# Experts' second weights: a load from HBM by SP in place of a copy on chip by GpSimd

## The chip, the cores and the metric

One core of one Trainium2 chip. The metric is the device time of one launch in microseconds (us), median of several runs. Engines are named as in the profile: PE (TensorE, matmuls), PEld (its weight loads), DVE (VectorE), ACT (ScalarE), POOL (GpSimd) and SP (SyncE, which here only issues DMAs).

## The reference

One layer in float32 over x (2, 1024, 256). A convolution and delta-rule attention with a gate over five paths comes first, then a gated recurrence over the 1024 steps gives h for 2048 tokens. The change lies in the last part, a feed-forward layer of eight experts, of which each token takes one:

```python
logits = xf @ gate_w.T + gate_b
top1 = jnp.argmax(logits, axis=-1)
for e in range(n_experts):                # 8
    h = jax.nn.relu(xf @ w1[e].T + b1[e])  # w1[e]: 1024 x 256
    y = h @ w2[e].T + b2[e]                # w2[e]: 256 x 1024
    out = out + jnp.where((top1 == e)[:, None], y, 0)
x = x + out
```

## The kernel before

The parts run one after the other, each a block of programs, one per engine, tied by semaphores written out by hand. `recur` (from about 599 us) computes h, and SP loads during it the experts' first weights `m.w1` (eight DMAs of 1 MB, line 1593) and two of the second ones `m.w2` (line 1595), and near its end four more of w2 (line 1603). All weights of all eight experts lie in SBUF when the blocks of tokens run.

`experts` (from 760.6 us) sorts the tokens by expert. DVE works out each token's place, PE turns h into rows, ACT copies them to `row` (line 2031), and SP writes the 16 tiles of rows to HBM as `h_rows` (line 1879), each when ACT has it. The sorted tokens are cut in 20 blocks (`BLOCKS`) of 128. A block has two halves of 64 tokens, and each half has one expert, whose number stands in `eid_i[0, 2g]` and `eid_i[0, 2g+1]` (cast at line 2117). The token list, `slot_token`, is cast at line 2124.

For block g:

- POOL gathers 128 rows of h (`fetch_x`, line 1908) and of the residual (`fetch_z`, line 1916) by indirect DMAs, and scatters the result (line 1929).
- PE turns the gathered rows (`turn_in`, line 1971), DVE copies them to `xt` (line 2139).
- PE computes the hidden layer (`hidden`, lines 1982 and 1985): per 512 columns and 128 inputs two matmuls that run side by side, tokens of the first half against `m.w1` at a register's expert, tokens of the second half against `w1_copy[g % 2]`, a room of one expert's weights in the tile h, which is no longer needed when h has been turned.
- DVE copies the hidden layer (line 2146), PE turns it (`turn_hidden`, line 2008), ACT applies bias and relu (line 2041), PE computes the output (`output`, lines 1996 and 1999), whose second half reads `w2_copy[g % 2]`, copied by DVE (line 2133). DVE adds residual and bias (lines 2154 and 2157).

`w1_copy` has two buffers. POOL fills them by `copy_w1(g)` (line 1893): wait until hidden(g-2) is done, load the expert's number into a register, copy 128 x 2048 floats from `m.w1`. PE's `hidden(g)` waits for `w1_copied` to reach g+1. The order on PE is hidden(g), turn_in(g+1), output(g-1), turn_hidden(g). The order on POOL is, once per g: fetch_x(g+3), copy_w1(g+2), wait for y of block g, scatter(g), fetch_z(g+2). Ahead of the loop stand copy_w1(0), the waits for the token list and for all rows of h in HBM, fetch_x(0), fetch_x(1), fetch_z(0), fetch_z(1), fetch_x(2), copy_w1(1). SP has nothing to do after the last row of h. DVE's first copy_w2 also waits for the rows in HBM. `keep_clock` is a helper (line 50) that gives PE matmuls of no use while it would wait.

Of the kernel before, what the change touches and what calls it, by code (L numbers as in the profile page):

```python
# [19 lines left out]
P = 128  # L20
# [15 lines left out]
E, EH = 8, 1024  # L36
# [3 lines left out]
BLOCKS = (B * T // HALF + E) // 2  # L40
# [1764 lines left out]
def experts(nc, d, m, out):  # L1805
# [9 lines left out]
    TILES = TOK // P  # L1815
    K2 = EH // P
    with ExitStack() as own:  # L1817
        sb = lambda n, s: own.enter_context(nc.sbuf_tensor("moe_" + n, s, F32))
        sem = lambda n: m.whole.enter_context(nc.semaphore("moe_" + n))
# [25 lines left out]
        eid_i = own.enter_context(nc.sbuf_tensor("eid_i", [1, 2 * BLOCKS], I32))  # L1845
        row = free_zw.rearrange("p (a n) -> p a n", n=D)
        w2_copy = free_zw[:, 0:2 * K2 * D].rearrange("p (i k n) -> p i k n", i=2, k=K2)
        w1_copy = m.h[:].rearrange("p j t -> p (j t)")[:, 0:2 * C * EH].rearrange("p (i c n) -> p i c n", i=2, c=C)
# [11 lines left out]
        names = ("zeros", "rows_out", "cleared", "r", "count_psum", "slots_ready", "slot_psum",  # L1860
                 "tokens_ready", "eid_ready", "turned", "row_ready", "picked", "x_psum", "xt_ready", "hid_psum", "hid_ready",
                 "ht_psum", "ht_ready", "y_psum", "y_half", "y_ready",
                 "w1_copied", "w2_copied")
        s = namedtuple("ExpertSemaphores", names)(*(sem(n) for n in names))
        x_in = [sem(f"x_in{i}") for i in range(2)]
        z_in = [sem(f"z_in{i}") for i in range(2)]
        y_done = [sem(f"y_done{i}") for i in range(2)]
        TURNED, TURNED_LAST = 2, 2
        out_rows = out.rearrange("b t d -> (b t) d")
# [3 lines left out]
        @block.sync  # L1873
        def _(sp):
            for e in (W2_AHEAD + 2, W2_AHEAD + 3):
                sp.dma_start(w2[:, e], d.w2T[e].rearrange("(k p) n -> p k n", p=P)).then_inc(m.w2_in, 16)
            for a in range(TILES):
                sp.wait_ge(s.row_ready, a + 1)
                sp.dma_start(m.h_rows[a * P:(a + 1) * P, :], row[:, a, :]).then_inc(s.rows_out, 16)

        @block.gpsimd
        def _(pool):
            for x in (*xin, *zin):
                nc.gpsimd.memset(x[:], 0.0).then_inc(s.cleared, 1)
            pool.wait_ge(s.cleared, 4)

            def copy_w1(g):
                if g >= BLOCKS:
                    return
                if g >= 2:  # L1890
                    pool.wait_ge(s.hid_psum, 2 * (g - 1))
                e = pool.value_load(eid_i[0:1, 2 * g + 1:2 * g + 2], min_val=0, max_val=E - 1)
                nc.gpsimd.tensor_copy(w1_copy[:, g % 2], m.w1[:, bass.ds(e, 1)].rearrange("p o c n -> p (o c) n")).then_inc(s.w1_copied, 1)

            pool.wait_ge(s.turned, TILES)
            pool.wait_ge(s.eid_ready, 1)
            copy_w1(0)
            pool.wait_ge(s.tokens_ready, 1)
            pool.wait_ge(s.rows_out, 16 * TILES)

            slots = lambda g: bass.IndirectOffsetOnAxis(ap=slot_token[:, g:g + 1], axis=0)

            def fetch_x(g):
                if g >= BLOCKS:
                    return
                if g >= 2:
                    pool.wait_ge(s.x_psum, g - 1)
                nc.gpsimd.indirect_dma_start(out=xin[g % 2][:], out_offset=None, in_=m.h_rows, in_offset=slots(g),
                                             bounds_check=TOK - 1, oob_is_err=False).then_inc(x_in[g % 2], 16)

            def fetch_z(g):
                if g >= BLOCKS:
                    return
                if g >= 2:
                    pool.wait_ge(s.y_half, g - 1)
                nc.gpsimd.indirect_dma_start(out=zin[g % 2][:], out_offset=None, in_=m.z_rows, in_offset=slots(g),
                                             bounds_check=TOK - 1, oob_is_err=False).then_inc(z_in[g % 2], 16)

            fetch_x(0)
            fetch_x(1)  # L1920
            fetch_z(0)
            fetch_z(1)
            fetch_x(2)
            copy_w1(1)
            for g in range(BLOCKS):
                fetch_x(g + 3)
                copy_w1(g + 2)
                pool.wait_ge(s.y_ready, 2 * (g + 1))
                nc.gpsimd.indirect_dma_start(out=out_rows, out_offset=slots(g), in_=y[g % 2][:], in_offset=None,  # L1929
                                             bounds_check=TOK - 1, oob_is_err=False).then_inc(y_done[g % 2], 16)  # L1930
                fetch_z(g + 2)
            for i in range(2):
                pool.wait_ge(y_done[i], 16 * ((BLOCKS + 1 - i) // 2))

        @block.tensor
        def _(pe):
# [36 lines left out]

            def hidden(g, e):
                pe.wait_ge(s.xt_ready, g + 1)
                pe.wait_ge(s.w1_copied, g + 1)
                for n in range(EH // N):
                    cols = slice(n * N, (n + 1) * N)
                    if g:
                        pe.wait_ge(s.hid_ready, 2 * (g - 1) + n + 1)  # L1980
                    for c in range(C):
                        nc.tensor.matmul(hid_bank[n][side(0), :], xt[:, c, side(0)],  # L1982
                                         m.w1[:, bass.ds(e, 1), c, cols].rearrange("p o n -> p (o n)"),
                                         start=(c == 0), stop=(c == C - 1), skip_group_check=True)
                        last = nc.tensor.matmul(hid_bank[n][side(1), :], xt[:, c, side(1)], w1_copy[:, g % 2, c, cols],  # L1985
                                                start=(c == 0), stop=(c == C - 1), skip_group_check=True)
                    last.then_inc(s.hid_psum, 1)
# [25 lines left out]

            turn_in(0)
            hidden(0, expert(0))
            turn_in(1)
            turn_hidden(0)
            pe.wait_ge(m.w2_in, 16 * (E - W2_AHEAD))
            for g in range(1, BLOCKS):
                hidden(g, expert(g))  # L2020
                if g + 1 < BLOCKS:
                    turn_in(g + 1)
                output(g - 1, expert(g - 1))
                turn_hidden(g)
# [186 lines left out]
def layer_kernel(nc, ins, out):  # L2211
    d = namedtuple("Inputs", ins)(**ins)
    with ExitStack() as ctx:
# [64 lines left out]
        m.h_rows = nc.dram_tensor("h_rows", (B * T, D), F32).ap()  # L2278
        recur(nc, d, m)
        experts(nc, d, m, out)  # L2280

# [35 lines left out]
```

## Time and profile before

| | us |
|---|---|
| median of 3 runs | 965.83 |
| lowest and highest | 963.97, 968.57 |
| the profiled execution | 969.41 |
| its span, first to last instruction | 967.6 |
| mean granted clock of PE, share of full | 0.873 |
| PE busy | 719.3 (74%) |
| DVE busy | 681.5 (70%) |
| ACT busy | 531.1 (55%) |
| POOL busy | 284.4 (29%) |
| DMA, mean over the span | 63 GB/s |

The profile is of one execution. Busy shares are means over the span, and here the parts of the kernel have different limits. So it is read by stretch: a table of stretches tells which engine is full, the chain that ended last tells what that stretch waits for, and the instructions in order of time tell how early each thing is ready. Times below are us from the start of the span.

### The profile page before, as it was taken

The page shows a single profiled execution, that of the slowest core. Times are in us where ns is not written, and L with a number is a line of the kernel's source. Part 1 is how long each engine was busy: PE and PEld are TensorE (multiplying, and loading weights), DVE is VectorE, ACT ScalarE, POOL GpSimd, SP SyncE. Part 2 cuts the span into 40 slices and gives each one's busy share as a digit, 9 for nine tenths or more (in the row PEclk, how much of TensorE's full clock was granted, in tenths as well). Part 3 has the DMA queues.
Part 4 walks back from the last instruction along what each step waited for, and adds up shares of the span by engine and source line. Part 5 has one row for each costly group of instructions (what it writes and reads, how often), then busy time and mean ns, then how long its engine had stood idle before and what let it go on. Part 6 is the DMA issues. An engine that isn't in the chain of part 4 may idle for free. (4 is left out here: it accounts for less than half of the span.)

```text
span 967.6 us, 16500 instructions
## 1 busy us (share of the span) xinstructions
PE 719.3 (74%) x6146; PEld 419.8 (43%) x6146; DVE 681.5 (70%) x958; ACT 531.1 (55%) x978; POOL 284.4 (29%) x238
## 2 busy tenths in 40 slices
PE   3850008886766547786598697999998989999995
PEld 1320004432545547775354254444444844445542
DVE  4999985967844798446679782799999734545442
ACT  5888854653423433555445345999999214443332
POOL 0000000000201000000033400699999156566661
PEclk9985557988899758899788899999999699999998
DMA  5640000000894000100300002920000911111100
GB/s 203 217 143 0 0 0 23 1 0 0 223 245 97 4 2 3 25 3 3 111 1 1 11 22 78 393 83 0 1 0 1 337 42 46 39 43 36 45 26 6
DMA packets 35473, 60.78 MB, mean 63 GB/s; under 512 B 7771, under 2 KB 22107, under 8 KB 35010
## 3 DMA queue, kind: packets, MB, share of 16 engines
q1 hardware_dynamic: 32514, 53.42, 17.6%
q0 software_dynamic: 2880, 6.30, 2.2%
q8 instruction: 50, 0.82, 0.4%
q14 instruction: 29, 0.24, 0.1%
HBM read 54.46 MB, written 6.82 MB: 63 GB/s over the span
## 5 line engine op out<-in xcount | busy, mean ns | idle before, releaser
L2041 ACT ACTIVATE xT<-x_tr,moe_b 128x64 f32<-128x64 f32 x320 | 67.6, 360 | 115.5 <-PE x_tr L2008 115.5
L1982 PE MATMUL x_hid<-w,moe_xt 128*64 x160 | 74.6, 610 | 0.8 <-DVE moe_xt L2139 0.6
L1985 PE MATMUL x_hid<-h,moe_xt 128*64 128x512 f32 x160 | 74.6, 610 | 0.0
L1996 PE MATMUL x_y<-w,xT 128*64 x320 | 73.3, 382 | 1.8 <-ACT xT L2041 1.8
L1999 PE MATMUL x_y<-hs,xT 128*64 128x256 f32 x320 | 73.3, 382 | 0.0
L1756 DVE TENSOR_TENSOR_SCAN w<-r_bank,w 128x512 f32<-128x512 f32 x56 | 69.6, 1246 | 3.2 <-POOL w L1716 3.2
L1170 POOL TENSOR_TENSOR path<-path,mix_pr 128x1280 f32<-128x1280 f32 x12 | 28.7, 2421 | 132.9 <-DVE mix_pr L1405 132.9
L224 PE MATMUL bad_sum<-spike_bad,ones 128*128 128x16 f32 x2 | 0.6, 384 | 83.9 <-ACT spike_outside L190 83.9
L1624 PE MATMUL r_bank<-recur_h_other,w1h 128*128 128x512 f32 x128 | 60.2, 592 | 0.2 <-ACT recur_h_other L1665 0.2
L1618 PE MATMUL r_bank<-hs,eye 128*128 128x512 f32 x112 | 57.2, 592 | 1.2 <-PEq L1099 1.2
L1716 POOL TENSOR_TENSOR w<-w,recur_h_other 128x512 f32<-128x512 f32 x32 | 37.7, 1180 | 65.6 <-ACT recur_h_other L1665 59.6
L220 PE MATMUL w_bank<-spike_wbuf,spike_pick 128*128 128x512 f32 x80 | 39.5, 654 | 23.4 <-DMA spike_wbuf<-in_gW 23.4
L482 DVE SCALAR_TENSOR_TENSOR proj_y<-proj_pre,mix_st,proj_y 128x1024 f32<-128x1024 f32 x36 | 46.2, 1285 | 11.0 <-ACT proj_y L445 9.8
L1996 PEld LDWEIGHTS x_y<-w,xT 128*64 128x64 f32 x320 | 42.3, 137 | 25.7 <-issue 5.6
L2154 DVE TENSOR_TENSOR moe_y<-x_y,moe_zin 128x256 f32<-128x256 f32 x20 | 8.5, 425 | 60.9 <-PE x_y L1999 60.9
L397 PE MATMUL pj<-hs,mix_st 128*128 128x512 f32 x96 | 46.3, 629 | 2.3 <-PEq L72 2.3
L2146 DVE COPY xT<-x_hid 128x512 f32<-128x512 f32 x40 | 27.7, 691 | 28.1 <-PE x_hid L1985 28.1
L1929 POOL DMA_INDIRECT out<-moe_y,slot_token x20 | 26.6, 1328 | 65.0 <-DVE moe_y L2157 65.0
L1624 PE MATMUL r_bank<-h,w1h 128*128 128x512 f32 x96 | 45.1, 592 | 0.0
L656 DVE COPY path<-fir_z_bank 64x256 f32<-64x256 f32 x64 | 27.0, 422 | 25.0 <-PE fir_z_bank L591 23.4
L419 POOL MEMSET proj_pre<- 128x6 f32 x1 | 0.1, 104 | 146.1 <-POOLq L72 146.1
L1688 ACT ACTIVATE r_bank<-r_bank,recur_leak,recur_leak_neg 128x512 f32<-128x512 f32 x56 | 42.0, 751 | 1.9
(297 smaller groups left out, 2006.4 us busy)
## 6 DMA issues: line engine op xcount, KB each, us to landing
spike_wbuf<-in_gW SPq DMA_DIRECT2D x8, 1280.0 KB, 6.4
w<-in_w1T SPq DMA_DIRECT2D x8, 1024.0 KB, 12.1
w<-in_w2T SPq DMA_DIRECT2D x8, 1024.0 KB, 9.0
fir_band<-in_band_l SPq DMA_DIRECT2D x11, 512.0 KB
fir_band<-in_band_m SPq DMA_DIRECT2D x11, 312.0 KB
mix_st<-in_band_l SPq DMA_DIRECT2D x5, 512.0 KB
xT<-in_xT SPq DMA_DIRECT2D x4, 512.0 KB, 6.4
xT<-in_xT SPq DMA_DIRECT2D x2, 1024.0 KB, 6.2
```

Source lines behind the costliest of these rows:

```text
L220: last = nc.tensor.matmul(w_bank[:], pick[:, at:at + P], wbuf[:, ch % 2, i, :], start=(ch == 0 and i == 0), stop=(ch == CHUNKS - 1 and i = ...
L397: last = nc.tensor.matmul(pj[u % 2][:, n * N:(n + 1) * N], w[:, i, k, c * P:(c + 1) * P], m.hs[:, k * B + b, n * N:(n + 1) * N], start=(k ...
L482: nc.vector.scalar_tensor_tensor(out, pre[:, u % 2, k:k + T], wc[:, i, c, k:k + 1], out, ALU.mult, ALU.add).then_inc(conv_step if k < KQ - ...
L1618: nc.tensor.matmul(out, m.eye[:], zw[:, c * B + b, t0:t0 + N], start=True, stop=False)
L1624: last = nc.tensor.matmul(out, wg[:, k, c * P:(c + 1) * P], state[u // UNITS % 2][:, k * B + b, t0:t0 + N], start=False, stop=(k == C - 1))
L1688: nc.scalar.activation(out, out, ACT.Identity, bias=leak[:, c:c + 1], scale=leak_neg[:, c:c + 1]).then_inc(s.j_ready, 1)
L1756: nc.vector.tensor_tensor_scan(change[:, r, :], j_bank[u % RING][:], rest[:, r, :], first, ALU.mult, ALU.add).then_inc(s.change_ready, 1)
L1982: nc.tensor.matmul(hid_bank[n][side(0), :], xt[:, c, side(0)], m.w1[:, bass.ds(e, 1), c, cols].rearrange("p o n -> p (o n)"), start=(c == ...
L1985: last = nc.tensor.matmul(hid_bank[n][side(1), :], xt[:, c, side(1)], w1_copy[:, g % 2, c, cols], start=(c == 0), stop=(c == C - 1), skip_ ...
L1996: nc.tensor.matmul(y_bank[side(0), :], ht[:, k, side(0)], w2[:, bass.ds(e, 1), k, :].rearrange("p o n -> p (o n)"), start=(k == 0), stop=( ...
L1999: last = nc.tensor.matmul(y_bank[side(1), :], ht[:, k, side(1)], w2_copy[:, g % 2, k, :], start=(k == 0), stop=(k == K2 - 1), skip_group_c ...
L2041: nc.scalar.activation(ht[:, k, side(x)], turned[:, side(x)], ACT.Relu, bias=b1[:, bass.ds(e[x], 1), k]).then_inc(s.ht_ready, 1)
```

## The change

POOL's `copy_w1` is taken out. SP, after its last row of h, waits until h has been turned and the experts' numbers are there, and then for each of the 20 blocks waits until hidden(g-2) is done, loads the number of the second half's expert into a register, and issues a DMA of that expert's whole w1 (256 x 1024 floats, 1 MB) from HBM to `w1_copy[g % 2]`. `w1_copied` becomes two semaphores, one per buffer, each raised by 16 per DMA, and PE waits on the one of its buffer. `m.w1`, read by the first half, is still loaded as before.

```diff
+        w1_copied = [sem(f"w1_copied{i}") for i in range(2)]
...
         @block.sync
...
+            sp.wait_ge(s.turned, TILES)
+            sp.wait_ge(s.eid_ready, 1)
+            for g in range(BLOCKS):
+                if g >= 2:
+                    sp.wait_ge(s.hid_psum, 2 * (g - 1))
+                e = sp.value_load(eid_i[0:1, 2 * g + 1:2 * g + 2], min_val=0, max_val=E - 1)
+                sp.dma_start(w1_copy[:, g % 2], d.w1T[bass.ds(e, 1)].rearrange("o (c p) n -> p (o c) n", p=P)).then_inc(w1_copied[g % 2], 16)
 
         @block.gpsimd
...
-            def copy_w1(g):
-                if g >= BLOCKS:
-                    return
-                if g >= 2:
-                    pool.wait_ge(s.hid_psum, 2 * (g - 1))
-                e = pool.value_load(eid_i[0:1, 2 * g + 1:2 * g + 2], min_val=0, max_val=E - 1)
-                nc.gpsimd.tensor_copy(w1_copy[:, g % 2], m.w1[:, bass.ds(e, 1)].rearrange("p o c n -> p (o c) n")).then_inc(s.w1_copied, 1)
-
-            pool.wait_ge(s.turned, TILES)
-            pool.wait_ge(s.eid_ready, 1)
-            copy_w1(0)
             pool.wait_ge(s.tokens_ready, 1)
             pool.wait_ge(s.rows_out, 16 * TILES)
...
             fetch_x(2)
-            copy_w1(1)
             for g in range(BLOCKS):
                 fetch_x(g + 3)
-                copy_w1(g + 2)
                 pool.wait_ge(s.y_ready, 2 * (g + 1))
...
             def hidden(g, e):
                 pe.wait_ge(s.xt_ready, g + 1)
-                pe.wait_ge(s.w1_copied, g + 1)
+                pe.wait_ge(w1_copied[g % 2], 16 * (g // 2 + 1))
```

## Rows read from the trace of the kernel before

**Rows 1.** The page, part 1: busy time, share of the span, instructions.

```profile
PE 719.3 (74%) x6146; PEld 419.8 (43%) x6146; DVE 681.5 (70%) x958; ACT 531.1 (55%) x978; POOL 284.4 (29%) x238
```

**Rows 2.** A stretch of four blocks: its length, engines' busy us, PEclk, DMA share, GB/s.

```profile
834.00:868.00 34.00, 34.00 (x234) 17.26 (x232) 16.51 (x29) 13.20 (x65) 21.11 (x16) 1.00 0.15 44
```

**Rows 3.** Chain that ended last: start us, us, what; hidden(2), (8), (9).

```profile
798.39 0.57 PE x_hid L1982
...
849.87 0.57 PE x_hid L1982
...
858.45 0.57 PE x_hid L1982
```

**Rows 4.** Waits from 800 us on: engine, line, releaser; us, times, longest.

```profile
POOL out L1929 <- DVE moe_y L2157: 65.0, 20, 7.6
...
PE x_y L1996 <- ACT xT L2041: 1.8, 1, 1.8
```

**Rows 5.** Chain that ended last, from the last row of h to hidden(0).

```profile
772.46 4.06 DMA h_rows<-hs
...
777.48 4.10 DMA moe_xin<-h_rows,slot_token
...
782.73 0.82 PE x_hid L1982
```

**Rows 6.** Start of the experts, in order of time: start, us, instruction [idle before].

```profile
761.76 11.15 SPq L1879 DMA_DIRECT2D h_rows<-hs  x16
...
772.66 0.17 DVE L2117 CAST eid_i<-moe_eid 1x40 int32<-1x40 f32 x1
774.20 1.89 POOL L1893 COPY h<-w 128x2048 f32 x1 [12.52 <-issue]
...
774.97 1.16 DVE L2124 CAST slot_token<-moe_empty 128x20 int32<-128x20 f32 x1
...
777.48 2.24 POOL L1908 DMA_INDIRECT moe_xin<-h_rows,slot_token  x1 [1.39 <-DMA h_rows<-hs]
...
781.71 0.41 PE L1971 MATMUL x_x<-eye,moe_xin 128*128 128x128 f32 x2 [2.67 <-DMA moe_xin<-h_rows,slot_token]
```

**Rows 7.** Stretch of hidden(0), columns as in rows 2.

```profile
783.00:786.00 3.00, 3.00 (x10) 0.85 (x8) 1.12 (x1) 0.00 (x0) 2.69 (x3) 0.51 0.25 74
```

**Rows 8.** One block, in order of time: DVE's y(5) to copy(8).

```profile
840.31 0.42 DVE L2154 TENSOR_TENSOR moe_y<-x_y,moe_zin 128x256 f32<-128x256 f32 x1 [2.95 <-PE x_y L1999]
...
844.80 0.44 PE L1971 MATMUL x_x<-eye,moe_xin 128*128 128x128 f32 x2
845.59 1.01 POOL L1908 DMA_INDIRECT moe_xin<-h_rows,slot_token  x1 [0.31 <-issue]
846.60 1.90 POOL L1893 COPY h<-w 128x2048 f32 x1
```

**Rows 9.** Loads of 1 MB: issue ns and landing, of w1, then landing of w2.

```profile
L1593 SPq DMA_DIRECT2D w<-in_w1T x8: 434/484/2298, 603.5 to 608.2; - x8
...
DMA to landing us min/median/max: 5.1/12.1/18.2
...
DMA to landing us min/median/max: 5.4/8.0/10.7
```

**Rows 10.** Stretches with those loads, columns as in rows 2.

```profile
610.00:615.00 5.00, 5.00 (x13) 2.25 (x12) 2.11 (x3) 3.91 (x7) 3.34 (x4) 1.00 1.03 419
625.00:630.00 5.00, 5.00 (x13) 2.27 (x12) 4.93 (x7) 4.75 (x9) 4.63 (x5) 1.00 1.08 357
```

**Rows 11.** PE's matmuls of 512 columns, 605 to 634, then 800 to 950.

```profile
L1624 PE MATMUL r_bank<-h,w1h x21: 590/592/593, 620.7 to 633.6; 128*128 128x512 f32 x21
...
L1985 PE MATMUL x_hid<-h,moe_xt x141: 592/592/643, 799.7 to 947.2; 128*64 128x512 f32 x141
```

**Rows 12.** Stretches around the first gather, columns as in rows 2.

```profile
774.00:775.00 1.00, 1.00 (x11) 1.00 (x11) 0.39 (x3) 0.00 (x0) 0.80 (x1) 1.00 0.86 283
...
780.00:781.00 1.00, 0.00 (x0) 0.00 (x0) 0.00 (x0) 0.00 (x0) 0.98 (x1) 1.00 0.48 127
```

More of the change, by code:

```diff
@@ L1862, in experts @@
                  "ht_psum", "ht_ready", "y_psum", "y_half", "y_ready",
-                 "w1_copied", "w2_copied")
+                 "w2_copied")
         s = namedtuple("ExpertSemaphores", names)(*(sem(n) for n in names))
```

## The prediction

> **What bounds the kernel now.** The page comes first: TensorE (PE) is busy 74% of the span, GpSimd (POOL) 29% [rows 1]. An average over stages decides nothing, so I read the stage that the diff touches, the experts, which run from 760.6 us to the end. The table by stretch shows PE busy for all of a stretch of four blocks at full clock, with DMA at 15% [rows 2]. The chain of waits says the same: from one hidden product to the next it is PE work end to end, and hidden(g) starts every 8.58 us: hidden(8) at 849.87, hidden(9) at 858.45; from hidden(2) at 798.39 to hidden(9) there are 7 periods, 60.06 / 7 = 8.58 [rows 3]. In the waits from 800 us on, POOL waits for DVE's y (65.0 us in 20 waits), which itself follows PE, and PE's own longest wait is one of 1.8 us, near the end [rows 4]. So the 18 blocks from hidden(2) to the last cost 8.58 us each, and POOL's copies can only matter by making hidden wait, which they don't.
>
> Ahead of that lies a stretch that no engine fills, from the routing to hidden(0). There the chain goes: the last row of h to HBM, landed at 772.46 + 4.06 = 776.5; POOL's first gather at 777.48, landed 4.10 us later; transposes at 781.71; hidden(0) at 782.73 [rows 5, 6]. PE idles 2.67 us before 781.71 [rows 6], and after that its granted clock is 0.51, the lower level (1.2 of 2.4 GHz), from 783 to 786 us [rows 7].
>
> **The change part by part.**
>
> Removed from POOL: 20 copies of 128x2048, 1.9 us each [rows 6, 8], 38 us in all, with 20 waits and 20 register loads. What it frees on the path: nothing in the steady blocks. Copy(8) runs 846.60 to 848.49, hidden(8) starts at 849.87, 1.38 us later, and after each copy POOL waits for DVE's y before the scatter, 3.3 us on average [rows 3, 4, 8]. The gather x(9), the only POOL step on which PE soon waits, stands ahead of the copy in program order, at 845.59, so it doesn't move up. In the start, copy(0) runs 774.20 to 776.09, and DVE's cast of the token list takes 1.16 us beside it, where the cast of the expert numbers took 0.17 [rows 6]; without the copy the list is ready 0.99 us sooner, about 775.14. But POOL must also wait for the last row of h, landed 776.5, so this is hidden too: copy(0) ends 0.4 us before that landing. Had the rows come earlier, up to 0.99 us would be won. Sum of the removal: 0.
>
> Added to SP: 20 times a wait, a register load, and one DMA of 1 MB (1.05 million bytes). SP has nothing else after its last row of h, issued by 772.91 [rows 6], so what it waits for holds nobody up. The register load on SP isn't in the trace; POOL's, with its wait and dispatch, takes at most 774.20 - 772.83 = 1.37 us from the expert numbers to the copy [rows 6], and below nothing it can't go, being new work. Issuing takes 0.48 us at the median and 2.30 at most [rows 9].
>
> The transfer: 1.05 MB at the 357 to 419 GB/s of the stretch in which eight such loads ran [rows 10] is 2.5 to 2.9 us of data. From issue to landing those eight took 5.1 us (nothing ahead of it) to 18.2, median 12.1 (several ahead) [rows 9]. Here one is in flight at a time, or two at the start, so I take 5.1 to 8.0, the latter the median of four w2 loads [rows 9].
>
> Steady blocks: the weights of block 9 may be fetched once hidden(7) has ended. Hidden(7) is over when the transposes for block 8 start at 844.80, and hidden(9) starts at 858.45, so 13.6 us are there [rows 3, 8]. Needed: 1.37 + 0.48 + 8.0 = 9.9 us by the dear ends, 6.9 by the cheap landing. Hidden with 3.7 us to spare. Cost 0.
>
> Beside other transfers: 20.97 MB more over the stage. In a block, 1.05 MB in 8.58 us is 122 GB/s on top of 44 [rows 2], under half of the 357 to 419 seen. The gather x(9) is issued 845.59 to 846.60 [rows 8]; the first gather landed 4.10 - 2.24 = 1.86 us after the end of its issue [rows 5, 6], so x(9) lands near 848.5 and is wanted one period after 844.80, at 853.38. Should a whole weight transfer go ahead of it, 2.9 us, it lands at 851.4, still 2 us early. Cost 0. The z gather of block 7 and the scatter of block 5 stand ahead of x(9) in POOL's order and must be done when DVE adds y(7), two periods after it added y(5) at 840.31, so at 857.5 [rows 8]: some 12 us.
>
> PE reading SBUF while DMA writes it: matmuls of 128x512 took 590 to 593 ns, median 592, in the stretch with DMA full [rows 10, 11], and the same 592 in the steady blocks [rows 11]. Cost 0, bound 0.
>
> The start is where the new transfers meet the path. SP gets past the expert numbers at 772.83, so weights(0) go out between 773.0 and 774.7 and weights(1) half a microsecond behind. The queue is still draining: 283 GB/s in 774 to 775 [rows 12]. Behind that come 2.1 MB, 5.0 to 5.9 us of data; begun between 775 and 776, they last to 780 to 781.9. Weights(0) land between 779.6 (774.5 + 5.1) and 782.5 (+ 8.0), and hidden(0) wants them at 782.73: just in time; by the 12.1 us it would be 786.6, 3.9 late. The gather x(0) moves its data from about 780.4, after its issue began to yield at 780 [rows 12], so it meets the tail of weights(1). It may lose nothing, or up to the 2.9 us of one whole transfer; I take 0.8 us, nearly the time for which the two overlap (780.4 to about 781.2, near the middle of the range just given), on the assumption that two queues share the engines evenly. Weights(1) are wanted at 789.74 and land by 785.
>
> PE's clock: the half-clock stretch made four pairs of matmuls take 0.82 us each, twice what they take at full clock [rows 5, 7]: 4 x 0.82 / 2 = 1.6 us. A later x(0) lengthens the idle ahead of it. The stretch may stay (0), last as long again (+1.6) or fall elsewhere and vanish (-1.6). The nearest row, an idle of 2.67 us followed by it, says it stays: 0.
>
> Sum: 0 (steady) + 0 (copies) + 0.8 (x(0) behind weights(1)) = +0.8 us. The profiled execution took 969.41 us (span 967.6, 1.8 around it), so it would be 970.2; that execution was 3.6 above the median of the runs, 965.83, to which I add the same 0.8: **966.6 us**.
>
> On turns between queues the Trainium skill has a rule that speaks against this change (DMA: Bandwidth & Descriptors, "Queues, rings and completion order"): a DMA engine changes queues only after a whole packet, and a completion mark lands only after all earlier writes of its engine, whatever their queue. No row of before has a gather beside a load; by that rule x(0) would lose more than my 0.8 us, up to the whole remaining transfer, the second rival below.
>
> **The rivals.**
>
> 1. Weights late in every block (slower). With two buffers hidden(g) can't start before hidden(g-2) has ended plus L, the time from there to landing. While L is under 13.6 us it costs nothing; above, (L - 13.6) / 2 per block over 18 blocks. For it: the median landing of eight in a row, 12.1, with the dearest issue and load gives 12.1 + 2.30 + 1.37 = 15.8, so 1.1 x 18 = 19.6 us, 985.4 us. Against: that median had others ahead of it, the free one took 5.1. It passes 0.5% (4.8 us) from L = 14.1 on.
>
> 2. A gather waits out a whole transfer. At the start 2.9 in place of 0.8: 968.7 us. In steady blocks it stays hidden, as above. This is the mechanism by which the rule just named would act.
>
> 3. Start dearer still: weights(0) 3.9 us late, with 1.6 us of clock: 971.3 us. For it: the queue is full until 775.
>
> 4. Faster: copies were in the way after all, by the port that POOL and DVE seem to share (the cast of 1.16 us). At most 0.99 us at the start, plus 1.6 if the slow clock goes: 963.2. In the steady blocks PE waits for no one [rows 2, 4]. This can't pass 0.5%.
>
> 5. The change doesn't do what it says: the weights of expert e come to the same place in the same order, only the source differs; if a load by a register took SP's queue longer than a fixed one, it would be seen as rival 1.
>
> **How the numbers follow.** Forecast (within about 1.5 us of 966.6): 0.58. Rival 2: 0.16. Rival 3: 0.08. Rival 4: 0.08. Rival 1: 0.10. About 0.5%, 4.8 us, is what a measurement of this kernel can tell from no change. Forecast, rival 2 and rival 4 lie within it (0.82); rival 3 at +5.5 lies just outside, and its costs may come smaller, so half of it is slower (0.04); of rival 1, 0.08 is slower and 0.02 too small to tell. The three runs of before spread from 963.97 to 968.57, so a median can stray by 2 us: 0.04 of rival 4 goes to faster. Slower 0.08 + 0.04 = 0.12, faster 0.04, same 0.84. The range reaches from rival 4, 963.2 rounded down to 963.0, to rival 3, 971.3, and leaves out rival 1 and the tails.
>
> **What would show it.** Period: hidden(g) every 8.58 us in the chain; if it is longer, and PE's waits name the weights' DMA, rival 1; if they name the gather, the 2 us of slack was wrong. Landing: 5.1 to 8.0 us in the DMA view. Start: x(0) should land near 782.4 in place of 781.6, hidden(0) start 0.8 later, with no PE wait on weights(0). POOL's busy time should be 38 us less and its wait for y longer by as much. Matmuls should stay at 592 ns. The prediction is wrong if the start moves by over 5 us, or if a longer idle of PE brings a slow clock into further blocks.

## The result, and the profile after

| | before | after |
|---|---|---|
| median of 20 runs, us | 965.47 | 969.95 |
| lowest and highest | 963.79, 970.15 | 964.99, 974.14 |
| the profiled execution | 969.41 | 970.06 |
| its span | 967.6 | 967.7 |

The changed kernel takes 1.0044 times as long, 95% interval 1.0031 to 1.0058: 3.0 to 5.6 us more. Two further sets of 12 runs gave 1.0019 (0.9996 to 1.0043) and 1.0032 (1.0012 to 1.0052). Weighted by their runs the three give 1.0034, some 3.3 us. So the changed kernel is slower, by about a third of a percent; the upper end of the first interval is 0.58%.

The weights that the change moves are w1 of the expert of a block's second half; the "second weights" of the title are these, not w2.

The two profiled executions differ by far less than the medians, because the one of before was a late one of its kind (969.41 against a median of 965.47) and because parts that the change doesn't touch differ by PE's clock (from 300 to 400 us PE was granted 0.74 in the one and 0.80 in the other). So single executions are poor witnesses of the whole. What can be compared is a stretch with fixed ends: from the first count matmul of the experts (line 1948 before, 1943 after) to hidden(2), where the steady blocks begin. I call it **the start**. In the kernel before it takes 798.39 - 762.31 = 36.1 us, in the changed one 798.52 - 761.58 = 36.9.

One part of the cost lies outside every profile. The device time of a run is longer than its span: by 1.8 us on average in the kernel before, and by 2.3 us in the changed one. The profile, from first to last instruction, doesn't see these 0.5 us. They are there in all nine kernels of this document in which POOL copies no weights (2.2 to 2.3 us), and in none of the five, the kernel before among them, in which it copies some (1.8 us). What they are isn't known.

In what follows, hidden(0) is a row of eight **pairs** of matmuls, one for each half of the block's tokens, side by side. A pair takes 0.42 us at full clock and 0.84 at the lower level; the first of a block takes longer (0.64 and 1.11).

The chain that ended last, of the changed kernel, start us, us, what (beside rows 5):

```profile
771.92 4.22 DMA h_rows<-hs
...
777.13 4.90 DMA moe_xin<-h_rows,slot_token
...
798.52 0.57 PE x_hid L1977
807.10 0.57 PE x_hid L1977
```

The last row of h lands in 4.22 us, against 4.06. The first gather, x(0), takes 4.90 us, against 4.10. The period, from one hidden product to the next, is 807.10 - 798.52 = 8.58, unchanged. Instructions in order of time, of the changed kernel (beside rows 6):

```profile
761.58 0.80 PE L1943 MATMUL x_hid<-moe_hot,moe_before 128*128 128x128 f32 x2 [0.56 <-DVE moe_hot L2052]
...
774.23 0.18 DVE L2119 CAST slot_token<-moe_empty 128x20 int32<-128x20 f32 x1
777.02 1.23 DVE L2128 COPY hs<-w 128x2048 f32 x1 [2.61 <-DMA h_rows<-hs]
777.13 2.21 POOL L1905 DMA_INDIRECT moe_xin<-h_rows,slot_token  x1 [16.17 <-DMA h_rows<-hs]
...
782.17 0.41 PE L1966 MATMUL x_x<-eye,moe_xin 128*128 128x128 f32 x2 [3.85 <-DMA moe_xin<-h_rows,slot_token]
```

The cast of the token list takes 0.18 us where it took 1.16, and POOL waits 16.17 us, until the rows have landed, all the same: this saving is hidden. PE idles 3.85 us ahead of x(0), against 2.67. DVE's copy of 1.23 us, right beside the gather's issue of 2.21 us, becomes a lead below.

The steady blocks, in three views of the changed kernel: four blocks as a stretch (columns as in rows 2), SP's loads as in rows 9, and SP's own waits (us in total, times, longest):

```profile
834.00:868.00 34.00, 34.00 (x232) 17.16 (x230) 16.50 (x29) 13.25 (x64) 13.47 (x12) 1.00 0.50 167
```

```profile
L1887 SPq DMA_DIRECT2D h<-in_w1T x20: 377/378/407, 773.5 to 931.6; - x20
...
DMA to landing us min/median/max: 4.8/5.4/6.7
```

```profile
SPq L1886 <- PE x_hid L1980: 136.9, 18, 13.1
```

PE is full, with DMA at 50% in place of 15% and POOL at 13.5 us in place of 21.1. The loads by a register are issued in 0.38 us and land 4.8 to 6.7 us after the issue began. SP spends 136.9 us in 18 waits for hidden(g-2), 7.6 us of every 8.58, so that it needs about 1.0 us from there to the end of its issue, 0.6 to its beginning. The weights are there some 6 us after hidden(g-2), with 13.6 to be had.

### The profile page after: what moved, and what is told of

Read it like the earlier page. It is cut to its first block and busy times, and to the rows that moved or that the text cites. A ratio compares the mean times of both kernels' runs of the same rounds, so it can differ in the third digit from the quotient of the medians.

```text
span 967.7 us, 16522 instructions
## 1 busy us (share of the span) xinstructions
PE 714.6 (74%) x6146; PEld 416.5 (43%) x6146; DVE 683.2 (71%) x958; ACT 530.6 (55%) x978; POOL 246.1 (25%) x218
## 5 line engine op out<-in xcount | busy, mean ns | idle before, releaser
L220 PE MATMUL w_bank<-spike_wbuf,spike_pick 128*128 128x512 f32 x80 | 39.6, 650 | 23.3 <-DMA spike_wbuf<-in_gW 23.3
L1994 PEld LDWEIGHTS x_y<-hs,xT 128*64 128x64 f32 x320 | 42.3, 137 | 0.0
```

Source lines behind the costliest of these rows:

```text
L220: last = nc.tensor.matmul(w_bank[:], pick[:, at:at + P], wbuf[:, ch % 2, i, :], start=(ch == 0 and i == 0), stop=(ch == CHUNKS - 1 and i = ...
L1994: last = nc.tensor.matmul(y_bank[side(1), :], ht[:, k, side(1)], w2_copy[:, g % 2, k, :], start=(k == 0), stop=(k == K2 - 1), skip_group_c ...
```

## The experiments

Three theories stood after the result. **S**: the cost lies in the start, where the gather x(0) meets the first two loads, and in PE's clock after the longer idle. **T**: the traffic in the steady blocks costs something. **C**: parts ahead of the experts run at another clock. Each ratio is against runs of the kernel before, taken on the same chip; the profile is of one execution. The first four kernels had 12 runs each on one chip.

**The changed kernel again.** No edit.

> The changed kernel itself, once more, for a second profile and a second ratio. Measured so far: 4.5 us slower by the medians (ratio 1.0044), while its one profile shows the experts only 0.9 us later against the kernel before (x(0) landing 4.90 us after its start in place of 4.10) and other parts of the kernel differing by PE's clock (0.80 in place of 0.74 between 300 and 400 us). Theory S (start): the cost lies between the last row of h and hidden(1), by the gather x(0) that shares the DMA engines with the first weights, and by PE's clock behind the longer idle; ratio again 1.003 to 1.006, and a profile in which that stretch is 1 to 5 us longer. Theory T (traffic): 20 MB more in the steady blocks cost something that the period doesn't show in the one profile; then a period over 8.58 us in some blocks. Theory C (clock elsewhere): parts ahead of the experts run at another mean clock in this kernel; ratio again 1.0044, with the experts at most 1 us longer.

Ratio 1.0019 (0.9996 to 1.0043). The clock of this execution (columns as in rows 2; the numbers behind the first comma are PE, PEld, DVE, ACT and POOL, then the granted clock of PE):

```profile
777.00:780.00 3.00, 0.00 (x0) 0.00 (x0) 0.00 (x0) 0.00 (x0) 2.29 (x3) 1.00 0.68 265
780.00:783.00 3.00, 1.73 (x6) 0.74 (x8) 1.32 (x2) 0.00 (x0) 1.61 (x2) 0.55 0.27 77
783.00:786.00 3.00, 3.00 (x10) 0.80 (x8) 0.70 (x2) 0.00 (x0) 0.48 (x1) 0.50 0.14 44
786.00:789.00 3.00, 3.00 (x15) 1.09 (x12) 1.17 (x3) 0.00 (x0) 0.00 (x0) 0.82 0.00 0
```

x(0) takes 5.95 us, 1.85 more than before, PE idles 4.46 us, and its clock is at the lower level from about 780.3 to 787.1, so that six pairs of hidden(0) run slow, where in the kernel before it was four. The start is 798.49 - 759.47 = 39.0 us, 2.9 more than before, as S expected; the ratio is below what S expected, with an interval wide enough for it.

**Loads in the steady blocks alone.** POOL keeps copy_w1(0) and copy_w1(1), and SP loads the rest. Against the changed kernel:

```diff
-            for g in range(BLOCKS):
+            for g in range(2, BLOCKS):        # SP; PE waits for POOL's copies while g < 2
```

> POOL copies the weights of blocks 0 and 1 as before, SP loads those of blocks 2 to 19. Theory S: ratio 1.000 (within 0.1%), the first gather lands 4.1 us after its start as before. Theory T: ratio 1.004. Theory C: anything between 1.000 and 1.005, with no change in the experts.

Ratio 1.001 (0.9996 to 1.0024); x(0) lands in 4.02 us, PE idles 2.81, the start is 793.93 - 757.72 = 36.2 us. Eighteen of the twenty loads cost nothing that the profile shows. The interval leaves room for 2.3 us, so it is not the ratio that speaks against T, but the profile: 8.58 us per block.

**Loads at the start alone.** The other half of the change: SP loads for blocks 0 and 1, and POOL copies for the others. Against the kernel before:

```diff
+            for g in range(2):                # SP
...
-            copy_w1(0)
-            copy_w1(1)
```

> SP loads the weights of blocks 0 and 1, POOL copies those of blocks 2 to 19 as before. Theory S: ratio 1.0044, as the whole change, x(0) landing 4.9 us after its start. Theory T: ratio 1.0005 (the 0.8 us of the gather alone). Theory C: as for the kernel above, no rule.

Ratio 1.0015 (0.9998 to 1.0032), between what S and T expected, 1.0044 and 1.0005, and with S's number outside the interval; but the changed kernel itself gave only 1.0019 on this chip. x(0) takes 5.03 us, and PE idles 3.56. Only three pairs ran slow, so that the start is 801.25 - 764.62 = 36.6 us, 0.5 more than before. The delay of the gather belongs to these two loads.

**Second load held back.** SP waits for x(0) ahead of weights(1).

```diff
             for g in range(BLOCKS):
+                if g == 1:
+                    sp.wait_ge(x_in[0], 16)
```

> The changed kernel, but SP issues the weights of block 1 only when the gather x(0) has landed. Theory S: weights(0) are through by 779, so x(0) lands 4.1 us after its start again, PE's idle ahead of the first transposes is 2.7 us, ratio 1.000; weights(1) land by 788, ahead of hidden(1) at 789.7. Theory T: ratio 1.004 all the same. Theory C: no rule.

Ratio 1.0002 (0.9984 to 1.002); x(0) in 3.99 us, idle 2.53, the start 793.01 - 757.08 = 35.9 us. One wait takes the gather's delay back, with all twenty loads still on SP: what x(0) met was weights(1). That it takes back the whole cost the ratios of this chip can't show (1.0002 against 1.0019, with intervals that overlap); against the three sets of the changed kernel together, 1.0034, they do. This is the plainest evidence for S.

The next four ran on another chip, in fewer runs: 5, 10, 10 and 4.

**More behind.** 1.5 MB of loads right behind weights(1), into rooms that are free then.

```diff
+                if g == 1:
+                    sp.wait_ge(s.slot_psum, 1)
+                    sp.dma_start(free_z[:, 0:C * EH] ..., d.w1T[0] ...).then_inc(more_in, 16)
+                    sp.dma_start(m.w1h[:], d.w1T[1][:, 0:HF] ...).then_inc(more_in, 16)
```

> The changed kernel, with 1.5 MB of loads more on SP's queue right behind the weights of block 1 (into rooms that nobody reads then; work added, nothing left out). The 3.5 MB then keep the DMA engines full until about 785.5, so that the gather x(0) lies wholly beside loads. 
Ratio 1.0059 (1.0039 to 1.0078).

```profile
777.69 7.01 DMA moe_xin<-h_rows,slot_token
```

```profile
778.00:781.00 3.00, 1.33 (x12) 1.14 (x11) 0.80 (x1) 0.00 (x0) 2.69 (x2) 1.00 1.02 408
781.00:784.00 3.00, 0.00 (x0) 0.00 (x0) 0.00 (x0) 0.00 (x0) 2.21 (x3) 0.91 1.03 411
784.00:787.00 3.00, 1.55 (x4) 0.59 (x6) 1.15 (x2) 0.00 (x0) 0.73 (x1) 0.50 0.87 316
```

The DMA engines are full through the whole flight of x(0), and it lands at 784.70, after 7.01 us, 2.91 more than in the kernel before. That is about the time of one whole 1 MB transfer (1.05 MB at the 408 and 411 GB/s of these rows is 2.6 us). It is neither the 5 to 6 us expected for turns of single descriptors nor the end of all loads, which go on after it. The Trainium skill's rule that an engine changes queues only after a whole packet (DMA: Bandwidth & Descriptors, "Queues, rings and completion order") would give such a wait; that a packet here is one load's share of an engine is my reading of the 2.91 us, not seen by itself. Whether the gather's data waited or only the mark of its completion, no run shows. The steady blocks say the same. There a gather of x and a load are issued at almost the same moment in each block, and in the changed kernel the gathers land like this:

```profile
L1905 POOL DMA_INDIRECT moe_xin<-h_rows,slot_token x20: 992/998/2211, 777.1 to 931.5; - x20
...
DMA to landing us min/median/max: 3.7/5.6/6.7
```

An issue of 1.0 and a flight of 1.86 us [rows 5, 6] make an estimated 2.9 without a load beside it, so that the median lost 2.7. The trace has no landing of a steady x gather without loads, but the gathers of z, of as many rows of the same size, landed in 2.8 us at the median in the kernel with loads at the start alone. PE wants x 7.8 us after its issue: hidden, but with 1.1 us to spare at the longest (0.7 where it took longest, 7.1 us, in the kernel with the second load held back).

**Filled.** The changed kernel with 38 pairs of filling matmuls in place of 20 while PE waits.

```diff
-            keep_clock(nc, m, spare_bank, 20)
+            keep_clock(nc, m, spare_bank, 38)
```

> The changed kernel, with 38 filling matmul pairs in place of 20 while PE waits for x(0), so that its idle of 3.85 us is nearly closed (18 x 0.24 = 4.2 us more). If the idle brings the slow clock of hidden(0), the first matmuls of hidden(0) take 0.42 us and not 0.84, the stretch from the count matmul to hidden(2) shrinks by 1.5 to 2 us, ratio about 1.000 to 1.002. If the slow clock comes from the light work itself, nothing changes.

Ratio 1.0004 (0.9983 to 1.0026). x(0) was late, 5.80 us, much as in the changed kernel's second profile, but PE idled 0.71 us and the clock never fell:

```profile
783.00:786.00 3.00, 3.00 (x18) 1.23 (x14) 1.42 (x3) 0.00 (x0) 0.27 (x1) 1.00 0.16 44
```

The start is 795.69 - 759.25 = 36.4 us against 39.0 there, with nearly the same lateness of the gather. Without the idle there are no slow pairs, and the start is 2.6 us shorter, of which 0.15 are the gather's own difference.

**DVE's order.** The second load held back, and DVE's first copies of w2 after hidden(0)'s copy.

```diff
-            dve.wait_ge(m.w2_in, 16 * (E - W2_AHEAD))
-            dve.wait_ge(s.rows_out, 16 * TILES)
-            copy_w2(0)
             x_out(0)
-            copy_w2(1)
             for g in range(BLOCKS):
                 hid_out(g)
                 if g + 1 < BLOCKS:
                     x_out(g + 1)
+                if g == 0:
+                    dve.wait_ge(m.w2_in, 16 * (E - W2_AHEAD))
+                    dve.wait_ge(s.rows_out, 16 * TILES)
+                    copy_w2(0)
+                    copy_w2(1)
```

> The changed kernel with weights(1) held back until x(0) has landed, and besides DVE's first two copies of w2 moved behind its copy of hidden(0). In all profiles so far POOL's first gather takes 2.2 us to issue beside DVE's copy of 1.23 us, later ones 1.0. If the copy is the reason, the issue takes 1.0, x(0) lands 2.8 us after its start, and the start is 1.2 us shorter: ratio 0.999. If not, 4.0 us as before.

Ratio 0.9995 (0.9972 to 1.0019), and in the profile:

```profile
772.15 1.22 POOL L1907 DMA_INDIRECT moe_xin<-h_rows,slot_token  x1 [15.99 <-DMA h_rows<-hs]
```

The issue takes 1.22 us where it took 2.2 beside DVE's copy; x(0) lands in 3.02, PE idles 1.79, no pair is slow, and the start is 790.39 - 756.78 = 33.6 us, twice the gain expected, since the slow pairs are gone as well. The Trainium skill (SBUF — State Buffer, "SBUF: two separate sides") says that GpSimd can't write the descriptors of its DMAs while DVE runs such a copy from SBUF to SBUF; the 1.0 us between the two issues agree.

**w2 later.** The same, and the last two loads of w2 behind weights(1), with PE's and DVE's waits for them moved to just ahead of their first use.

```diff
-            for e in (W2_AHEAD + 2, W2_AHEAD + 3):     # SP, ahead of the rows of h
-                sp.dma_start(w2[:, e], ...).then_inc(m.w2_in, 16)
...
+                if g == 1:                             # SP, after weights(1)
+                    for e in (W2_AHEAD + 2, W2_AHEAD + 3):
+                        sp.dma_start(w2[:, e], ...).then_inc(m.w2_in, 16)
```

> As the kernel before in this list, and besides the last two loads of w2 (2 MB), which stood ahead of the rows of h in SP's queue, go behind weights(1), with PE's and DVE's waits for them moved to just before their first use. The queue was full until 775.6, and the last row of h landed 4.1 us after its issue; with 2 MB less ahead it should land in 2.3 to 3, so another 1 to 1.7 us: ratio 0.997 in all, the first version faster than both kernels. If the loads then come too late for output(0), the gain is lost again.

Ratio 1.0064 (1.0038 to 1.0089): the gain was lost again and more. Among the waits between 745 and 800 us:

```profile
PE x_y L1994 <- DVE hs L2132: 4.9, 1, 4.9
```

The last row of h landed in 3.68 us, 0.4 less. But w2 landed 11.62 us after its issue. The DMA engines were full from 782 to 794 us (share 1.04 to 1.08), as I read it with weights(1) and weights(2) beside w2. output(0) waited 4.9 us, DVE's copy of w2 being late, and the clock behind that was 0.50 from 791 to 797 (the start is 40.3 us).

The last four ran on a third chip, 12 runs each.

**DVE's order without SP's loads.** The kernel before with only the reordering of DVE just shown.

> The kernel before (POOL's copies, no loads by SP), with DVE's first two copies of w2 behind its copy of hidden(0). If the gain of the start in the reordered changed kernel (x(0) landing 3.0 us after its start, no slow matmuls in hidden(0), 33.6 us from the count matmul to hidden(2) in place of 36.1) comes from DVE's order alone, it shows here as well: 33.4 to 34 us and a ratio of 0.997. If it needs POOL free of copies, the stretch stays above 35 us.

Ratio 0.9983 (0.9965 to 1.0001). x(0) in 3.00 us, idle 1.59, no slow pair, the start 795.48 - 762.05 = 33.4 us. The gain of the start is DVE's order, and needs nothing of SP's loads. The interval of the ratio just takes in no change.

**The same, w2 later.** Without SP's loads of w1; SP issues the last two w2 loads when x(0) has landed.

> As the kernel before in this list, and the last two loads of w2 issued by SP when x(0) has landed. In the version with SP's w1 loads this made output(0) wait 4.9 us, since 3 MB stood in the queue at once; here it is 2 MB alone, landed by 786, ahead of output(0) at 788. The last row of h then lands 3.7 us after its issue in place of 4.1: 33.0 us from the count matmul to hidden(2), ratio 0.9965. If output(0) still waits, 1 to 3 us more.

Ratio 0.9991 (0.9972 to 1.0009). The start is 794.39 - 760.00 = 34.4 us, a microsecond longer than without it, where 33.0 was expected. With 2 MB less ahead of the rows these land in 1.8 us at the median (3.7 at the longest), and POOL no longer waits for them but for the token list, whose cast takes 1.31 us beside copy_w1(0); and output(0) waits 1.3 us for w2, landed 9.24 us after its issue:

```profile
774.87 1.23 POOL L1909 DMA_INDIRECT moe_xin<-h_rows,slot_token  x1 [0.94 <-DVE slot_token L2126]
```

This is the place where the change under study could pay: with the rows early, the cast beside copy_w1(0) is what holds the first gather. A version with SP's weights(0), weights(1) and the w2 loads in an order that keeps x(0) clear and output(0) fed wasn't tried.

**The changed kernel, third time.**

> The changed kernel a third time. Theory S as it stands now: x(0) lands 0.8 to 1.9 us later than in the kernel before, PE's idle ahead of it is 3.8 to 4.5 us in place of 2.7, the slow stretch in hidden(0) takes 3 to 6 pairs of matmuls in place of 4; count matmul to hidden(2) 36.9 to 39.0 us in place of 36.1, ratio 1.002 to 1.0045. Theory C: the stretch is within 1 us of 36.1 and the ratio still over 1.003.

Ratio 1.0032 (1.0012 to 1.0052). x(0) in 4.69 us, 0.6 later than before, PE's idle 3.52 us, three slow pairs and one partly, the start 797.05 - 760.27 = 36.8 us. The gather, the idle and the start all lie just below what was expected, the ratio within it.

**DVE's order with SP's loads, second time.**

> The changed kernel with weights(1) held back and DVE's copies moved, a second time: 33.6 us from the count matmul to hidden(2), 2.5 less than in the kernel before, so a ratio of 0.9975 if nothing else differs; the first one gave 0.9995 with an interval of 0.25% either way. If this one lies above 1.000 again, some cost of SP's loads is missing from the account.

Ratio 0.9976 (0.996 to 0.9992), faster than both kernels of the case. Here x(0) again took 3.00 us and PE idled 1.80, as in the first, but the clock fell near 777.7, and three pairs were slow and two partly:

```profile
777.00:778.00 1.00, 1.00 (x6) 0.29 (x4) 0.00 (x0) 0.00 (x0) 0.69 (x2) 0.82 0.86 180
778.00:779.00 1.00, 1.00 (x6) 0.34 (x4) 0.00 (x0) 0.00 (x0) 0.74 (x1) 0.50 0.98 401
```

The start was 792.18 - 756.89 = 35.3 us, not the 33.6 expected. With the same idle of 1.8 us one execution kept its clock and the other lost it.

The starts of all profiles together:

| kernel | x(0), us | PE idle, us | start, us | ratio |
|---|---|---|---|---|
| before | 4.10 | 2.67 | 36.1 | |
| after | 4.90 | 3.85 | 36.9 | 1.0044 |
| after, again | 5.95 | 4.46 | 39.0 | 1.0019 |
| after, third time | 4.69 | 3.52 | 36.8 | 1.0032 |
| steady loads alone | 4.02 | 2.81 | 36.2 | 1.001 |
| first loads alone | 5.03 | 3.56 | 36.6 | 1.0015 |
| second load held back | 3.99 | 2.53 | 35.9 | 1.0002 |
| more behind | 7.01 | 5.51 | 39.6 | 1.0059 |
| filled | 5.80 | 0.71 | 36.4 | 1.0004 |
| DVE's order, load held back | 3.02 | 1.79 | 33.6 | 0.9995 |
| the same again | 3.00 | 1.80 | 35.3 | 0.9976 |
| w2 later | 3.22 | 1.31 | 40.3 | 1.0064 |
| DVE's order, no loads | 3.00 | 1.59 | 33.4 | 0.9983 |
| the same, w2 later | 3.01 | 1.3 | 34.4 | 0.9991 |

## Why the prediction was right, and where it was off

**The forecast** was 966.6 us in a range of 963.0 to 971.3, most likely too small a change to tell. Measured: 969.95, inside the range, slower by 0.44%, under the 0.5% set as the bound, which the interval (up to 0.58%) just passes. The forecast's own sum, +0.8 us, was too small: the ratio says +3.0 to +5.6. So the main reasons held, and the sum had only a part of the cost.

**The removal**, 0: right, and for the reason given. The cast of the token list took 0.98 us less, and POOL waited for the rows.

**The steady blocks**, 0: right. L was to be 6.9 to 9.9 us; it was about 6, and 13.6 were there. (The sum counted the issue twice, since landings are counted from the start of the issue, and took 1.37 us for wait and register load, which needed 0.6.) Rival 1 fell at once. The gather beside a load I had let pass behind a whole transfer as the worst case, landing 5.8 us after its issue; that is not the worst but the ordinary case (median 5.6, longest 6.7). The margin held, by less than the 2 us stated.

**The matmuls**, 0: right, 592 ns at the median as before.

**x(0) behind weights(1)**, 0.8 us: that the two meet was right, as the load held back shows, and the size was a little low. The four profiles with both loads ahead and nothing else changed there gave 0.8, 1.85, 0.6 and 0.9 us, 1.0 on average; with filling matmuls 1.7. The assumption of an even share was the weak one. Rival 2 named the other, a gather that waits out one transfer, at 2.9 us; with loads through its whole flight it lost 2.91. That weights(1) end sooner in the changed kernel, so that x(0) pays only what is left of the transfer, was not run by itself, but the traces bear it out. The earlier the gather follows SP's first load, the more it loses:

| kernel | from SP's first load to the gather's issue, us | the gather lost, us |
|---|---|---|
| after, again | 774.59 - 771.20 = 3.39 | 1.85 |
| filled | 774.78 - 771.39 = 3.39 | 1.70 |
| first loads alone | 779.75 - 776.19 = 3.56 | 0.93 |
| after | 777.13 - 773.52 = 3.61 | 0.80 |
| after, third time | 775.70 - 771.98 = 3.72 | 0.59 |

The gather is issued about 1 us after the last row of h has landed, and that landing moves by a third of a microsecond against the loads. With it the loss changes by 1.3 us; by an even share of the engines it should change by less than that third. With more loads behind and the same 777.69 - 774.30 = 3.39 us, it lost 2.91: then the loads didn't end before its turn.

**PE's clock**, 0, bounds +1.6 and -1.6: this term was the least sure, and it held in two of three profiles. Start less gather leaves 0.1 us in the first profile of the changed kernel and 0.1 in the third, but 1.1 in the second (2.9 - 1.85). I took the stretch of four slow pairs as fixed, since the nearest row showed it. It isn't: three, six and three pairs were slow in the three profiles, and none when the idle was filled. In the execution with six the clock cost something once more at the end, where output(19) waits for ACT: from hidden(2) to the end of the span it took 969.4 - 798.49 = 170.9 us against 169.2 in the kernel before (columns as in rows 2; in the kernel before PE's clock was 1.00 here):

```profile
956.00:960.00 4.00, 3.55 (x26) 1.97 (x22) 0.41 (x1) 0.00 (x0) 0.00 (x0) 0.78 0.01 4
```

Of the fourteen profiles only this one has these 1.7 us (the others take 169.1 to 169.6), so they aren't shown to belong to the change. The term belonged beside the first with its upper end: a delay of 0.6 to 1.9 us of a gather, plus 0 to 1.1 us of clock at the start.

**What the sum left out.** The forecast carried the 1.8 us around the span over unchanged. They were 2.3, so that 0.5 us was put at nothing without a reason.

**What stays open.** The three starts of the changed kernel are 0.9, 2.9 and 0.7 us longer than the one of before, 1.5 on average, and 0.5 lie outside the span, while the three ratios give some 3.3 us. The rest of about 1.3 us isn't located. The two halves of the change gave 1.001 and 1.0015, and both intervals reach down to no change. It may be chance, since the runs of one kernel in one set spread by 5 to 12 us and the starts by 2, or the clock at other waits, such as the one at the end just told; three profiles don't decide it. That the parts ahead of the experts run otherwise in this kernel (C) wasn't shown, and isn't excluded. Up to the first count matmul the three profiles take 761.6, 759.5 and 760.3 us against 762.3 before, and all fourteen lie between 756.8 and 764.6, too far apart to tell. The mean granted clock of the runs was that of the kernel before in one set (0.877) and lower in the other (0.875 against 0.878). The held-back load, with the same instructions on all engines but one wait, gave 1.0002, which speaks against C.

## What to carry to other kernels

Taking copies off an engine that has time doesn't help, and a load that replaces a copy meets whatever short transfer is on the path: look for the one moment when PE waits for a gather, and keep bulk loads out of the 3 us ahead of it and out of its flight, by a wait on that gather's own semaphore. Ask of a stall what PE's clock does after it, since an idle PE may pay as much again in slow matmuls, and fill the wait if you can't shorten it. And look which copy of DVE runs beside POOL's issue of the gather that everyone waits for: moving it took 2.7 us off the start of the kernel before (36.1 to 33.4), though the whole time fell by only 0.05 to 0.24% in the three sets that have it and w2 in its old place, one of them clear of no change. When parts of a sum don't add up to the measured difference, compare the device time with the span, too; a part of it can lie outside every profile.

## What the runs showed of the hardware that I had not expected

- A gather of 128 rows of 1 KB lost 2.91 us to a stream of 1 MB loads in another queue, about one load's 2.6 us of data, and 2.7 us at the median in the steady blocks (an estimated 2.9 without a load, 5.6 beside one).
- PE's clock after an idle isn't a function of the idle's length alone: after 1.8 us it stayed at 1.00 in one execution and fell to 0.50, some 2.3 us after work had resumed, in another; after 4.46 us it fell during the idle, and the next 6.4 us were slow.
- A load whose source is chosen by a register was issued in 0.38 us, and landed in 5.4 us at the median, no dearer than the fixed ones (5.1 with nothing ahead) [rows 9].
- Device time less span was 2.3 us in the nine kernels whose POOL copies no weights, and 1.8 in the five whose POOL does, whatever SP loads; the cause is open.
